# The sum of a token's row and its expert's second bias, made by GpSimd for 34 of 71 expert tiles

## The chip, the cores and the metric

The kernel runs on one core of a Trainium2 chip. The metric is the device time of one execution in microseconds (us); lower is better. Engine names in the profile: PE is TensorE (PEld its weight loads), DVE VectorE, ACT ScalarE, POOL GpSimd, SP SyncE, which only issues DMAs. A "q" behind a name (DVEq) is that engine's instruction queue.

## What is computed

64 sequences of 128 tokens, width 128, go through two layers; the last step is a mixture of 8 experts in which each token uses the expert of its largest router logit:

```python
    x = x + _L0_xattn_ref(ctx_1024, _layernorm(x, axis=-1), mask_BxS2_bk0, ...)
    x = x + _L0_ffn_ref(_layernorm(x, axis=-1), ...)
    x = x + _L1_xattn_ref(_layernorm(x, axis=-1), ctx_1024, L1_xattn_We, L1_xattn_W2)
    x = x + _L1_ffn_ref(_layernorm(x, axis=-1), ...)

    def _L1_ffn_ref(x, Wr, br, W1, b1, W2, b2):
        ...
        logits = xf @ Wr.T + br
        expert_idx = jnp.argmax(logits, axis=-1)
        h = jax.nn.relu(jnp.einsum('td,efd->etf', xf, W1) + b1[:, None, :])
        y = jnp.einsum('etf,edf->etd', h, W2) + b2[:, None, :]
        out = y[expert_idx, jnp.arange(xf.shape[0])]
```

The sum that the change moves is x + b2 of the token's expert, to which the second expert product is added later.

## The kernel before

**Rounds.** The program is written out in rounds j from -3 to 74; each engine has its own function `run` with its part of a round, in the order in which its queue executes it. In round j the cross-attention of sequence j is in several stages at once, and the dense parts of the later layers are done for groups of four sequences: rho = (j - 2) mod 4 tells which part of a group's work a round holds. From round 64 on (`tail`) no new sequence begins. Rounds 64 to 74 finish the last groups, and each holds three expert tiles besides.

**Expert tiles.** Tokens are scattered to DRAM sorted by expert (`sorted_rows`, by GpSimd's indirect DMA, line 810) and come back as 71 tiles of 128 tokens of one expert each (SyncE, line 502). The first 41 tiles come from sequences that are routed early; the other 30 are loaded when the last group's scatters have landed. One tile takes this way: VectorE's `prep` (lines 933 to 948) centres the tokens (L940), copies the expert's first weight and bias (L943) and adds the second bias to the row (L947, into one of eight buffers `xb2`); TensorE's `tile` transposes the tokens (L1641), makes h (L1647) and two tiles later y (L1655); ScalarE copies the transposed tokens (L554) and applies bias and relu (L559); VectorE's `finish` adds y and `xb2` into one of eight output buffers (L960); GpSimd's `store` sends the buffer to `out` by an indirect DMA (L800). `prep` works two tiles ahead of the number it is called with, `finish` and `store` two tiles behind it, so a tile's sum is made four places before it is used. In VectorE's queue the expert's number is read into a register by `look_up` (L931) one place earlier. Stores are numbered with semaphores, and the output buffer of tile k waits for the store of tile k - 8.

**The rstd chain.** Each round with layer norms in it makes one batch of 1/sqrt(var + eps): GpSimd writes the variances (`var_in`, L872), ScalarE takes ln and exp (L684, L687), GpSimd makes one Newton step (L881 to L887). In the tail it runs in rounds 64, 65, 66, 68, 69 and 72. ScalarE's `roots` stands ahead of the round's third expert tile in its queue. GpSimd's queue of a tail round is: variances, chain, in some rounds the centring `t_c` of a group (L835, L838), `xb` (L825), `ctx_now` (L820) or two scatters, and then the three stores.

After round 74 follow the tiles of `REST`, 32 and up, with nothing beside them.

Of the kernel before, what the change touches and what calls it, by code (L numbers as in the profile page):

```python
# [14 lines left out]
ALU = mybir.AluOpType  # L15
# [28 lines left out]
DEEP = 6  # L44
# [14 lines left out]
def whole(nc, x_res, ctx_res, ident, w1_all, w2_all, table, sent, padded, sorted_rows, out, x, ctx, mask,  # L59
# [3 lines left out]
    B, S, D = x.shape  # L63
# [5 lines left out]
    E, F = F1.shape[0], F1.shape[1]  # L69
# [6 lines left out]
    with ExitStack() as stack:  # L76
# [3 lines left out]
        def sem(name):  # L80
            return stack.enter_context(nc.semaphore(name))
# [115 lines left out]
        W1C, W2C, TOK = F + C, F + D, B * P  # L197
        out_rows = out.rearrange("b s d -> (b s) d")
        texp_i, trow_i = table["texp_i"], table["trow_i"]
        rows = x_res  # L200
# [6 lines left out]
        xb2 = [res[:, n * D:(n + 1) * D] for res in (q_t, o_n) for n in range(4)]  # L207
# [57 lines left out]
        sim_done = sem("sim_done")  # L265
# [6 lines left out]
        onT_done = sem("onT_done")  # L272
# [10 lines left out]
        second_in = sem("second_in")  # L283

        names = ("setup_d", "setup_t", "setup_c", "routed", "b_in", "wT_done", "w_copied", "w_taken", "tot_done", "tot_copied",
                 "a_bn", "a_mv", "fence_t", "lt_done", "lt_copied", "b_bn", "b_mv", "c_bn", "c_mv",
                 "ta_done", "amax_done", "step_done", "inv_done", "q1_done", "q2_done", "qT_done", "qt_copied",
                 "acc_done", "ya_done", "xb2_done", "x2_done", "tb_done", "tbT_done", "tb_copied",
                 "ctx_taken", "ctxT_done", "ctx_copied", "ke_done", "ke_copied", "v2_done",
# [2 lines left out]
                 "lmax_done", "ge_done", "cand_done", "cmax_done", "oh_done", "rank_done", "place_done", "gsum_done",  # L292
                 "own_done", "before_done", "slot_done", "staged")
        s = {n: sem("m_" + n) for n in names}
        tile_names = ("w1_set", "t_set", "T_done", "t_copied", "h_done", "relu_done", "y_done", "xb_set", "fin")
        se = {n: sem("e_" + n) for n in tile_names}
        out_sent = [sem(f"e_out_sent{n}") for n in range(STORES)]
        ld = [sem(f"e_ld{n}") for n in range(DEEP)]
# [7 lines left out]
        LAST = B + 10  # L306
# [86 lines left out]
        def group(g, inside):  # L393
            return inside or 0 <= g < NG
# [6 lines left out]
        def chain(j, inside):  # L401
            if inside or j <= B + 2:
                return j + 4
            return max([B + 6] + [n for at, n in CHAINS.items() if at <= j])

        def after(eng, name, g, inside):

            if inside or g >= 0:
                eng.wait_ge(s[name], g + 1)

        def grp(res, g, w=slice(0, D)):
            return res[:, bass.ds(G * g, G), w]
# [4 lines left out]
        TAIL, PLACES = B, 3  # L417
        TOTAL_AT, PAD_AT = 4 * (EARLY + 2) + 3, 4 * (NG + 1) + 3

        def tail(j, inside):  # L420
            return not inside and j >= TAIL

        def tile_no(j, place):

            return PLACES * (j - TAIL) + place - 1
# [3 lines left out]
        def has_tile(k):  # L429
            return 0 <= k < T  # L430

        def past(eng, name, k):
            if k >= 0:
                eng.wait_ge(se[name], k + 1)

        def flat(ap):
            return ap.rearrange("p a d -> p (a d)")
# [91 lines left out]
        def _(act):  # L529
# [18 lines left out]
            def tile(k, four=0, inside=False):  # L548
                if inside or has_tile(k + 1):

                    past(act, "T_done", k + 4 * four + 1)
                    if k == -1:
                        act.wait_ge(lo_done, B)
                    nc.scalar.activation(t_t[:, (k + 1) % 4, :], ps_t[(k + 1) % 2], ACT.Copy).then_inc(se["t_copied"], 1)  # L554
                if inside or has_tile(k):

                    past(act, "h_done", k + 4 * four)
                    for c in range(C):
                        last = nc.scalar.activation(h_t[k % 4][:, c, :], ps_h[k % 2][:, c * P:(c + 1) * P], ACT.Relu,  # L559
                                                    bias=w1_now[k % 4][:, F + c:F + c + 1])  # L560
                    last.then_inc(se["relu_done"], 1)
# [197 lines left out]
        def _(pool):  # L759
# [35 lines left out]
            def store(k):  # L795
                if has_tile(k - 2):

                    past(pool, "fin", k - 2)
                    n = (k - 2) % STORES
                    nc.gpsimd.indirect_dma_start(  # L800
                        out=out_rows,
                        out_offset=bass.IndirectOffsetOnAxis(ap=rows[:, k - 2, D + 2:D + 3].bitcast(U32), axis=0),
                        in_=o_now[:, n, :], in_offset=None, bounds_check=TOK - 1,
                        oob_is_err=False).then_inc(out_sent[n], 16)

            def scatter(g, lanes, inside):

                after(pool, "staged", g, inside)
                for i in lanes:
                    nc.gpsimd.indirect_dma_start(  # L810
                        out=sorted_rows, out_offset=bass.IndirectOffsetOnAxis(ap=idx[:, i:i + 1], axis=0),
                        in_=stage[:, i, :], in_offset=None).then_inc(sent[i // 2], 16)

            def run(j, par, rho, g, inside, pos, turn):
# [13 lines left out]
                if rho in (1, 2) and (inside or 0 <= g - 2 < NG - 1):  # L828
                    scatter(g - 2, (2 * rho - 2, 2 * rho - 1), inside)
                def centred(j, g):  # L830

                    after(pool, "tcT_done", g - 2, inside)
                    after(pool, "x3_done", g - 1, inside)
                    pool.wait_ge(rs_ready, chain(j, inside))
                    nc.gpsimd.tensor_tensor(t_c[:, :, :], grp(x_res, g - 1),  # L835
                                            stat_c[:, :, 0:1].to_broadcast([P, G, D]), ALU.subtract).then_inc(s["cc_done"], 1)
                    after(pool, "cc_done", g - 1, inside)
                    nc.gpsimd.tensor_tensor(t_c[:, :, :], t_c[:, :, :],  # L838
                                            rstd[:, j % 2 if tail(j, inside) else 1 - par, 28:28 + G].unsqueeze(2).to_broadcast([P, G, D]),
                                            ALU.mult).then_inc(s["tc_done"], 1)  # L840
# [61 lines left out]

                if rho == 2 and tail(j, inside) and group(g - 1, inside):
                    centred(j, g)
                if tail(j, inside):
                    store(tile_no(j, 0))
                    store(tile_no(j, 1))
                    if g - 2 == NG - 1 and rho == 0:
                        pool.wait_ge(padded, 16 * E)
                        scatter(g - 2, (0, 1), inside)  # L910
                    store(tile_no(j, 2))
                    if g - 2 == NG - 1 and rho == 0:
                        scatter(g - 2, (2, 3), inside)
                if not inside and 0 <= j < len(lots) - 3:
                    nc.gpsimd.memset(ctx_res[:, packed[j + 3], :], 0.0).then_inc(ctx_zeroed, 1)

            run(-3, 1, 3, -3, False, -3, 0)
            nc.gpsimd.memset(v_x[:, :, :, DH:DH + 1], 1.0).then_inc(setup_g, 1)
            nc.gpsimd.memset(v_c[:, :, :, DH:DH + 1], 1.0).then_inc(setup_g, 1)
            run(-2, 0, 0, -2, False, -2, 0)  # L920
            rounds_written_out(run)
            for k in REST:
                store(k)

        @block.vector
        def _(dve):
# [6 lines left out]
            def prep(k):  # L933
                if has_tile(k + 2):

                    n, e = (k + 2) % 4, number[k + 2]
                    past(dve, "T_done", k - 2)
                    dve.wait_ge(ld[(k + 2) % DEEP], 16 * ((k + 2) // DEEP + 1))
                    row = rows[:, k + 2, :]
                    nc.vector.tensor_scalar(t_now[:, n, :], row[:, 0:D], row[:, D:D + 1], row[:, D + 1:D + 2],  # L940
                                            ALU.subtract, ALU.mult).then_inc(se["t_set"], 1)
                    past(dve, "relu_done", k - 2)
                    nc.vector.tensor_copy(w1_now[n], flat(w1_all[:, bass.ds(e, 1), :])).then_inc(se["w1_set"], 1)  # L943
                    past(dve, "fin", k - 6)
                    if k == 2:
                        dve.wait_ge(onT_done, B)
                    nc.vector.tensor_tensor(xb2[(k + 2) % 8], row[:, 0:D], flat(w2_all[:, bass.ds(e, 1), F:W2C]),  # L947
                                            ALU.add).then_inc(se["xb_set"], 1)

            def finish(k):  # L950
                if has_tile(k - 2):

                    n = (k - 2) % STORES
                    if k - 2 >= STORES:
                        dve.wait_ge(out_sent[n], 16 * ((k - 2) // STORES))
                    if k == 2:
                        dve.wait_ge(pv_done, 2 * B)
                    past(dve, "xb_set", k - 2)
                    past(dve, "y_done", k - 2)
                    nc.vector.tensor_tensor(o_now[:, n, :], ps_y[k % 2], xb2[(k - 2) % 8], ALU.add).then_inc(se["fin"], 1)  # L960

# [948 lines left out]
```

## Time and profile before

| | |
|---|---|
| time, median of 3 runs | 921.79 us (919.71 to 922.56) |
| time of the profiled execution | 918.84 us |
| its span | 917.0 us |
| busy: PE, DVE, ACT, POOL | 96%, 81%, 75%, 48% |
| instructions of POOL | 1020 |
| granted TensorE clock | 0.999 of full |

The profile is of one execution. Its span runs from the first to the last recorded instruction; the 1.84 us between span and time lie around it. A busy share is a mean over the whole span: the expert tiles begin only near 747 us, and the engines' shares there are others. A time in a row is counted from the start of the span.

### The profile page before, as it was taken

Reading aid. Unit: us, or ns where it says so; the run is one execution under the profiler, and the core shown is the slowest. Engines: PE = TensorE matmul, PEld = TensorE weight load, DVE = VectorE, ACT = ScalarE, POOL = GpSimd, SP = SyncE. Lnnn points to the kernel's source line nnn. Section 1 sums busy time; section 2 is a strip of 40 time slices with the busy share of each in tenths; the row PEclk is TensorE's granted clock in tenths of the full one; section 3 lists DMA queues with packets and bytes.
Section 4 is the critical chain, followed back from the end, with each engine's and each line's share of the span. In section 5 each row is a group of like instructions: output and inputs, shape, how many; then the busy total and the mean of one; then the engine's idle time right before and its main releaser. Section 6 shows DMA issues by size and latency. Waiting matters only on the chain.

```text
span 917.0 us, 34057 instructions
## 1 busy us (share of the span) xinstructions
PE 882.9 (96%) x12822; PEld 782.1 (85%) x12822; DVE 747.0 (81%) x2654; ACT 686.8 (75%) x1671; POOL 437.0 (48%) x1020
## 2 busy tenths in 40 slices
PE   7999999999999999999999999999999989999997
PEld 6788888888888888888888888888888778898996
DVE  5667888888888888889888888898889878877553
ACT  4887778787878787878787878787877766776664
POOL 4422434354535453545354535453545355777554
PEclk9999999999999999999999999999999999999999
DMA  6753000000000000000000000000000023164310
GB/s 190 204 132 73 3 3 2 2 14 3 14 2 15 3 14 2 14 3 15 2 15 3 14 3 13 3 15 2 15 3 13 3 64 78 46 123 99 93 49 22
DMA packets 45206, 31.66 MB, mean 35 GB/s; under 512 B 11555, under 2 KB 40166, under 8 KB 45046
## 3 DMA queue, kind: packets, MB, share of 16 engines
q1 hardware_dynamic: 39398, 19.93, 9.2%
q0 software_dynamic: 4320, 8.50, 2.9%
q8 instruction: 105, 1.72, 0.8%
q10 hardware_dynamic: 1328, 1.06, 0.5%
q14 instruction: 55, 0.45, 0.2%
HBM read 17.75 MB, written 12.17 MB: 33 GB/s over the span
## 4 chain that ended last, share of the span: by engine, by line
PE 80%; DVE 11%; issue 2%; POOL 2%; DMA 1%; ACT 1%; SPq 1%; DVEq 0%; POOLq 0%; ACTq 0%
PE ps L1781 12%; PE ps L1733 11%; PE ps L1666 9%; PE ps L1706 6%; PE ps L1474 6%; PE ps L1476 6%; PE ps L1475 6%; PE ps L1655 5%; PE ps L1647 5%; PE ps L1805 4%; DVE sumsq L1286 2%; PE ps L1527 1%; PE ps L1551 1%; PE ps L1521 1%; PE ps L1676 1%
## 5 line engine op out<-in xcount | busy, mean ns | idle before, releaser
L1781 PE MATMUL ps<-qT_all,kT_all 64*64 64x128 f32 x4096 | 129.8, 273 | 8.3 <-DVE o_n L1378 6.6
L706 ACT ACTIVATE prob<-ps,neg_shift 128x512 f32<-128x512 f32 x128 | 80.9, 682 | 62.5 <-PE ps L1781 62.5
L1733 PE MATMUL ps<-v_x,prob 128*64 128x65 f32 x2048 | 126.2, 225 | 0.2 <-ACT probs L626 0.2
L1781 PEld LDWEIGHTS ps<-qT_all,kT_all 64*64 64x64 f32 x4096 | 110.8, 133 | 16.4 <-DVE o_n L1378 9.3
L1733 PE MATMUL ps<-v_c,prob 128*64 128x65 f32 x2048 | 123.0, 222 | 0.0
L1398 DVE TENSOR_TENSOR qk_hat<-ps,rstd 128x512 f32<-128x512 f32 x168 | 106.2, 683 | 19.4 <-POOL rstd L887 19.0
L1286 DVE TENSOR_REDUCE sumsq<-qk_hat 128x8 f32<-128x512 f32 x168 | 106.9, 675 | 18.3 <-ACT qk_hat L639 17.8
L1474 PE MATMUL ps<-w_hi,xc_hi 128*128 128x512 f32 x272 | 113.9, 419 | 0.8 <-POOL xc_lo L853 0.8
L881 POOL TENSOR_TENSOR rs_t<-rs_y 128x32 f32<-128x32 f32 x73 | 17.7, 243 | 201.5 <-ACT rs_y L687 201.5
L1733 PEld LDWEIGHTS ps<-v_x,prob 128*64 128x64 f32 x2048 | 103.6, 138 | 11.8 <-issue 11.3
L1476 PE MATMUL ps<-w_hi,xc_lo 128*128 128x512 f32 x272 | 107.4, 395 | 0.0
L1475 PE MATMUL ps<-w_lo,xc_hi 128*128 128x512 f32 x272 | 107.2, 394 | 0.0
L1733 PEld LDWEIGHTS ps<-v_c,prob 128*64 128x64 f32 x2048 | 103.6, 138 | 0.0
L639 ACT ACTIVATE qk_hat<-ps 128x512 f32<-128x512 f32 x168 | 97.0, 608 | 7.4 <-PE ps L1476 1.4
L1666 PE MATMUL ps<-ident,qk_hat 128*128 128x128 f32 x672 | 95.2, 277 | 3.1 <-DVE qk_hat L1398 2.7
L800 POOL DMA_INDIRECT out_dram<-prob,x_res x71 | 72.0, 1014 | 43.1 <-DVE prob L960 28.2
L1666 PEld LDWEIGHTS ps<-ident,qk_hat 128*128 128x128 f32 x672 | 74.1, 141 | 15.0 <-issue 10.0
L706 ACT ACTIVATE prob<-ps,mask_now 128x512 f32<-128x512 f32 x128 | 80.6, 685 | 0.7 <-PE ps L1781 0.7
L810 POOL DMA_INDIRECT sorted_rows<-stage,idx x64 | 71.8, 1121 | 15.9 <-issue 14.6
L896 POOL TENSOR_TENSOR x_b<-x_res,lno_b 128x128 f32<-128x128 f32 x64 | 33.7, 526 | 94.2 <-DVE x_res L1417 94.2
L1655 PE MATMUL ps<-w_all,kT_all 128*128 x568 | 74.7, 275 | 0.0
L1706 PE MATMUL ps<-wo_sb,o_t 128*128 128x128 f32 x512 | 69.8, 279 | 1.5 <-issue 1.5
(241 smaller groups left out, 2207.4 us busy)
## 6 DMA issues: line engine op xcount, KB each, us to landing
x_res<-sorted_rows SPq DMA_DIRECT2D x71, 65.5 KB
w_all<-in_L_ffn_W_dram SPq DMA_DIRECT2D x16, 256.0 KB, 5.6
sorted_rows<-fill SPq DMA_DIRECT2D x8, 327.5 KB
out_dram<-prob,x_res POOLq DMA_INDIRECT x71
sorted_rows<-stage,idx POOLq DMA_INDIRECT x64, 2.4
ctx_res<-in_ctx_dram SPq DMA_DIRECT2D x8, 115.5 KB
x_res<-in_x_dram SPq DMA_DIRECT2D x1, 768.0 KB
sorted_rows<-fill SPq DMA_DIRECT2D x1, 524.0 KB, 5.2
```

The lines of the kernel that those rows point to most:

```text
L639: nc.scalar.activation(sq[:, n * INNER:(n + 1) * INNER], ps_qk[:, n, :], ACT.Square).then_inc(sq_done, 1 if n == 0 or fresh(pos + 1) else 2)
L706: nc.scalar.activation(prob[:, n // 2, n % 2 * INNER:(n % 2 + 1) * INNER], ps_s[n], ACT.Exp, bias=(mask_now[:, par:par + 1] if n > 1 else ...
L1286: nc.vector.reduce_sum(sumsq[:, n * H:(n + 1) * H], sq[:, n * INNER:(n + 1) * INNER].rearrange("p (h d) -> p h d", d=DH), AX).then_inc(ss_ ...
L1398: nc.vector.tensor_tensor(qk_hat[:, n * INNER:(n + 1) * INNER].rearrange("p (h d) -> p h d", d=DH), ps_qk[:, n, :].rearrange("p (h d) -> p ...
L1474: nc.tensor.matmul(dst, tok_hi, w_hi[:, w:w + INNER], start=True, stop=False)
L1475: nc.tensor.matmul(dst, tok_hi, w_lo[:, w:w + INNER], start=False, stop=False)
L1476: return nc.tensor.matmul(dst, tok_lo, w_hi[:, w:w + INNER], start=False, stop=True)
L1655: last = nc.tensor.matmul(ps_y[k % 2], h_t[(k - 2) % 4][:, c, :], flat(w2_all[:, bass.ds(e, 1), c * P:(c + 1) * P]), start=c == 0, stop=c ...
L1666: last = nc.tensor.transpose(ps_qk[:, n, t * P:(t + 1) * P], qk_hat[:, n * INNER + t * P:n * INNER + (t + 1) * P], ident[:, :])
L1706: last = nc.tensor.matmul(ps_o(j, inside), o_t[:, t * P:(t + 1) * P], wo_sb[:, t, :], start=t == 0, stop=t == PAIRS - 1)
L1733: last = nc.tensor.matmul(dst[half:half + DH, :], prob[:, kt, col + half:col + half + DH], v, start=kt == 0, stop=kt == 1)
L1781: last = nc.tensor.matmul(ps_s[2 * kt + half][key:key + DH, cols], keys, q_t[rows, cols], start=True, stop=True)
```

## The change

GpSimd gets a function `with_bias(k)`: for the tiles 0 to 33 it waits for the loaded rows and for the tile that last used the buffer, reads the expert's number into a register and makes the sum. In a tail round it is called behind each of the three stores, for the tile that lies four after the stored one; the sum of tile 0 is made ahead of them in round 64. VectorE's `prep` makes the sum only from tile 34 on, with a semaphore of its own, `xb_more`, and `finish` waits for the one or the other. Buffers, order of tiles and all other work are as before.

```diff
-                 "a_bn", "a_mv", "fence_t", "lt_done", "lt_copied", "b_bn", "b_mv", "c_bn", "c_mv",
+                 "a_bn", "a_mv", "lt_done", "lt_copied", "b_bn", "b_mv", "c_bn", "c_mv",
...
-        tile_names = ("w1_set", "t_set", "T_done", "t_copied", "h_done", "relu_done", "y_done", "xb_set", "fin")
+        tile_names = ("w1_set", "t_set", "T_done", "t_copied", "h_done", "relu_done", "y_done", "xb_set", "xb_more", "fin")
...
+        BY_POOL = PLACES * (LAST + 1 - TAIL) + 1
+
+        def biased(eng, k):
+
+            if 0 <= k < BY_POOL:
+                eng.wait_ge(se["xb_set"], k + 1)
+            elif k >= BY_POOL:
+                eng.wait_ge(se["xb_more"], k + 1 - BY_POOL)
...
+            def with_bias(k):
+                if has_tile(k) and k < BY_POOL:
+
+                    pool.wait_ge(ld[k % DEEP], 16 * (k // DEEP + 1))
+                    past(pool, "fin", k - 8)
+                    if k == 4:
+                        pool.wait_ge(onT_done, B)
+                    e = pool.value_load(texp_i[0:1, k:k + 1], min_val=0, max_val=E - 1)
+                    nc.gpsimd.tensor_tensor(xb2[k % 8], rows[:, k, 0:D], flat(w2_all[:, bass.ds(e, 1), F:W2C]),
+                                            ALU.add).then_inc(se["xb_set"], 1)
...
+                if not inside and j == TAIL:
+                    pool.wait_ge(sim_done, 4 * B)
+                    with_bias(0)
                 if tail(j, inside):
                     store(tile_no(j, 0))
+                    with_bias(tile_no(j, 0) + 2)
                     store(tile_no(j, 1))
+                    with_bias(tile_no(j, 1) + 2)
                     if g - 2 == NG - 1 and rho == 0:
                         pool.wait_ge(padded, 16 * E)
                         scatter(g - 2, (0, 1), inside)
                     store(tile_no(j, 2))
+                    with_bias(tile_no(j, 2) + 2)
...
-                    past(dve, "fin", k - 6)
-                    if k == 2:
-                        dve.wait_ge(onT_done, B)
-                    nc.vector.tensor_tensor(xb2[(k + 2) % 8], row[:, 0:D], flat(w2_all[:, bass.ds(e, 1), F:W2C]),
-                                            ALU.add).then_inc(se["xb_set"], 1)
+                    if k + 2 >= BY_POOL:
+                        past(dve, "fin", k - 6)
+                        nc.vector.tensor_tensor(xb2[(k + 2) % 8], row[:, 0:D], flat(w2_all[:, bass.ds(e, 1), F:W2C]),
+                                                ALU.add).then_inc(se["xb_more"], 1)
...
-                    past(dve, "xb_set", k - 2)
+                    biased(dve, k - 2)
```

## Rows read from the trace of the kernel before

**Rows 1.** Busy us by engine (with instruction counts), granted clock, in stretches of the span.

```profile
775.00:800.00 25.00, 22.15 (x195) 20.55 (x194) 20.78 (x72) 17.65 (x69) 19.42 (x27) 1.00 0.20 55
...
850.00:875.00 25.00, 25.00 (x227) 25.00 (x226) 14.42 (x55) 17.15 (x67) 11.64 (x13) 1.00 0.37 95
```

**Rows 2.** Waits, 765 to 800 us: engine and line, releaser, total us, times, longest.

```profile
ACT rs_ln L684 <- POOL var_in L872: 2.8, 2, 2.2
...
PE ps L1641 <- DVE xc_hat L940: 1.3, 2, 0.8
```

**Rows 3.** Chain that ended last, 765 to 815 us: start, us, what.

```profile
796.99 0.23 POOL var_in L872
...
798.04 1.16 PE ps L1647 x8
```

**Rows 4.** ScalarE's timeline: start, us, line, operation, in brackets the idle time before.

```profile
797.24 0.23 ACT L684 ACTIVATE rs_ln<-var_in 128x32 f32<-128x32 f32 x1 [2.17 <-POOL var_in L872]
...
818.76 0.26 ACT L554 ACTIVATE xc_t<-ps 128x128 f32<-128x128 f32 x1
```

**Rows 5.** GpSimd's timeline, 764 to 834 us, columns as before.

```profile
764.90 0.25 POOL L887 TENSOR_TENSOR rstd<-rs_t,rs_y 128x32 f32<-128x32 f32 x1
765.64 1.04 POOL L800 DMA_INDIRECT out_dram<-prob,x_res  x1 [0.48 <-issue]
...
768.30 0.98 POOL L800 DMA_INDIRECT out_dram<-prob,x_res  x1 [0.30 <-issue]
769.28 0.23 POOL L872 TENSOR_TENSOR var_in<-stat_a,var_add 128x4 f32<-128x4 f32 x1
771.18 0.24 POOL L881 TENSOR_TENSOR rs_t<-rs_y 128x32 f32<-128x32 f32 x1 [1.67 <-ACT rs_y L687]
...
784.15 1.20 POOL L825 TENSOR_TENSOR xb<-x_res,bias_b 128x512 f32<-128x512 f32 x1
785.52 0.99 POOL L810 DMA_INDIRECT sorted_rows<-stage,idx  x1 [0.17 <-issue]
...
814.21 0.97 POOL L800 DMA_INDIRECT out_dram<-prob,x_res  x1 [1.20 <-DVE prob L960]
...
833.84 1.03 POOL L810 DMA_INDIRECT sorted_rows<-stage,idx  x1 [0.80 <-DVE idx L1232]
```

**Rows 6.** TensorE's timeline, 819 to 850 us (instructions of one line merged).

```profile
819.52 1.06 PE L1647 MATMUL ps<-xc_t,w_more 128*128 128x128 f32 x8
...
833.14 0.33 PE L1641 MATMUL ps<-ident,xc_hat 128*128 128x128 f32 x1 [0.56 <-issue]
...
840.01 0.33 PE L1641 MATMUL ps<-ident,xc_hat 128*128 128x128 f32 x1 [0.92 <-DVE xc_hat L940]
...
849.55 0.27 PE L1641 MATMUL ps<-ident,xc_hat 128*128 128x128 f32 x1
```

**Rows 7.** VectorE's timeline, 746 to 784 us.

```profile
746.72 0.46 DVE L940 TENSOR_SCALAR xc_hat<-x_res 128x128 f32<-128x128 f32 x1 [1.28 <-DMA x_res<-sorted_rows]
...
747.43 0.28 DVE L947 TENSOR_TENSOR qT_all<-x_res,w_all 128x128 f32<-128x128 f32 x1
747.64 0.28 DVE L1308 BATCH_NORM_STATS2 o<-ps 128x6 f32<-128x128 f32 x1
...
750.28 0.43 DVE L1143 TENSOR_SCALAR q_bf<-q_round 128x512 bf16<-128x512 f32 x1
...
783.59 2.06 DVE L1143 TENSOR_SCALAR q_bf<-q_round 128x512 bf16<-128x512 f32 x1
```

**Rows 8.** GpSimd's groups by form over the span: busy us, mean ns, idle before.

```profile
L896 POOL TENSOR_TENSOR x_b<-x_res,lno_b 128x128 f32<-128x128 f32 x64 | 33.7, 526 | 94.2 <-DVE x_res L1417 94.2
```

**Rows 9.** Register loads of VectorE's queue at line 931: duration ns min/median/max.

```profile
L931 DVEq TENSOR_LOAD <-table_texp_i x71: 298/304/957, 745.1 to 901.5; - x71
```

**Rows 10.** SyncE's timeline, 800 to 860 us.

```profile
842.39 16.85 SPq L502 DMA_DIRECT2D x_res<-sorted_rows  x15
```

**Rows 11.** DMA issues by line: KB each, median us from issue to landing.

```profile
tb_t<-in_L_xattn_We_dram SPq DMA_DIRECT2D x1, 64.0 KB, 2.1
```

## The prediction, made before the changed kernel ran

> **What bounds the kernel now.** I read the busy shares by stretch first. In the last stretch of pure expert tiles TensorE is busy all the time; in 775 to 800 us, where three expert tiles a round are woven into the last dense groups, it is at 22.15 of 25 us, VectorE at 20.78 and GpSimd at 19.42 [rows 1]. GpSimd's average over the whole kernel (48%) says nothing about this place. Next the waits of 765 to 800 us: ScalarE's logarithm of the rstd chain waits 2.8 us for GpSimd's var_in, 2.2 us of it at once, and TensorE waits 1.3 us for VectorE's centred tokens [rows 2]. Then the chain that ended last: it walks through var_in on GpSimd at 796.99, ln and exp on ScalarE after its wait of 2.17 us, and the next tile's weight product on TensorE at 798.04 [rows 3, 4]. The last question is what GpSimd does ahead of that var_in, and its timeline answers it: from the var_in of round 66 at 769.28 to the one of round 69 at 796.99 it goes from one instruction straight to the next [rows 3, 5]. Its only real waits there are the 1.67 us at 771.18 and a ScalarE round trip of 0.7. The 0.30 us marked "issue" between two indirect DMAs is no free time; each pair of them has it, whatever else happens. It meets VectorE again only at 814.21, where it waits 1.20 us for a finished tile.
>
> So in rounds 66 to 69 GpSimd ends last, at rounds 70 to 72 it has about 0.9 us in hand (1.20 at 814.21 less the usual 0.30 [rows 5]), and before 763 and from 828 to 840 VectorE is late: TensorE has gaps of 0.56 and 0.92 us there [rows 6]. From 840 on TensorE alone counts.
>
> **What is taken away.** 34 additions on VectorE (L947). One takes 0.28 us in its row, but the next instruction starts 0.21 after it (747.43 to 747.64), so each is worth 0.21 [rows 7]: 34 x 0.21 = 7.1 us of VectorE. It counts only where VectorE is late. Before 763 it starts the first stores about 0.5 us earlier: five additions are worth 1.05, and a wait for TensorE in their middle eats half; this is an estimate from the same rows. From 828 to 840 six additions are 1.3 us and the two gaps of TensorE are 1.48 [rows 6]; I take 1.0. In between, other engines end last, and it buys nothing.
>
> **What is added.** On GpSimd 34 additions of 128x128 f32, with a register load each. The nearest row of that addition is x_b, the same form with two SBUF inputs: 526 ns mean [rows 8]. What it adds to the queue is another number. A short tensor instruction (0.25 us at 764.90) is followed by an indirect DMA 0.74 us after its own start; a long one (1.20 at 784.15) is followed after 0.17 [rows 5]. So an addition of about 0.5 takes 0.74 before the next store and removes the 0.30 gap: 0.44. The third of each round mostly goes ahead of a tensor instruction, which follows a DMA with no gap (768.30 + 0.98 = 769.28): 0.53. Sum 1.4 a round if the register load hides. On VectorE's queue that load is 304 ns [rows 9], and two of them in the open held VectorE for 1.28 us ahead of 746.72 [rows 7], though the row puts it down to a DMA. So the load costs between 0 and 0.64 each. Since tensor instructions follow a DMA without a gap, the queue runs ahead, and I take nearly the lower end: 0.5 an addition in all, 1.5 us a round. Bounds 1.2 and 3.2 a round; a gain is excluded, for no row shows GpSimd doing two things at once. The waits on the loaded rows and on the tile eight before cost nothing: a store just ahead has already waited for the tile four before.
>
> **Where it lands.** Behind an addition in the queue stand the stores and the scatters of the round, and the next round's var_in, the rstd chain and t_c. Round 64: four additions after 757.04, when GpSimd is waiting for VectorE's statistics up to 762.38; free. Round 65: var_in at 769.28 - 0.5 + 1.5 = 770.3; ScalarE is ready for it at 770.5, and the rs_t at 771.18 hardly moves [rows 5]; 0. Rounds 66, 67, 68: 3 x 1.5 = 4.5 us, all of it in the var_in of round 69. TensorE is only about 0.1 us from waiting there, as its product at 798.04 starts right behind ScalarE's copy [rows 3]. Delay 4.5. Rounds 69, 70, 71: another 4.5, less the 0.9 in hand: the var_in of round 72 is 8.1 late. TensorE has 0.5 there (ScalarE's copy ends at 819.02, the product starts at 819.52) [rows 4, 6]: delay 7.6. VectorE's gain from 828 to 840 takes off 1.0: 6.6. Then the end of the routing: nine additions of rounds 72 to 74 stand ahead of the last scatter, 4.5 less the 0.5 that the scatter at 833.84 waits for VectorE beyond the usual [rows 5]: 8.1 + 4.0 = 12.1 us late. The load of tile 41 is issued at 842.39 behind it [rows 10], so at 854.5; 64 KB have landed in 2.1 us [rows 11], in other rows in up to 3.1: 856.6. VectorE needs 0.34 for it, and TensorE wants it at 849.55 + 6.6 = 856.2 [rows 6]: 0.8 more. Sum: 4.5 + 4.5 - 0.9 - 0.5 - 1.0 + 0.8 = +7.4 us.
>
> The profiled execution has a span of 917.0 and a time of 918.84, so 926.2 for the changed kernel; the median of the runs shown, 921.79, stands 2.95 above the profiled execution, and I carry that over: 921.79 + 7.4 = 929.2. With 1.2 us a round the sum is 6 x 1.2 - 2.4 = +4.8 (no wait for the load), with 1.8 it is 8.4 and about 2 for the load, +10.4. The new wait of VectorE, on an addition by GpSimd, stands ahead of the last addition of each tile, with the preparation of later tiles queued behind it. An addition is issued after the store of the tile four before; with GpSimd some 8 us late, the sum for tile 25 comes about 1.4 us after VectorE asks for it. That is 0 to 1.4 on top and in the range.
>
> **The shared port.** The q_bf conversion on VectorE took 2.06 us at 783.59 while GpSimd's xb addition ran from 784.15 to 785.35; its like at 750.28 took 0.43 [rows 5, 7]. So a VectorE instruction can be held for all of a GpSimd one. The Trainium skill, SBUF — State Buffer, section "SBUF: two separate sides", says that the two engines share a port pair as an exclusive lock, for VectorE instructions with two SBUF inputs or in a two-port mode: the trace agrees at this place. By that rule each moved addition can hold VectorE for up to its own length, and the change would give back its 1.5 us of gain; the sum would be 8.9 in place of 7.4. The rows alone leave open how many of the additions meet such an instruction: none of the sum above needs it, and both values lie inside the forecast.
>
> **Rivals.** (1) GpSimd's register load lies open. Each addition then costs 0.44 + 0.64, 3.2 a round. The var_in of round 66 is 1.45 late already, the sum is 1.45 + 6 x 3.2 - 2.4 = 18.3, and the load of tile 41 comes some 6 us after that: +24, 946 us. For it: the two open loads on VectorE. Against: the queue running ahead of a 0.97 us DMA. (2) Faster: GpSimd's additions fit into time that I count as busy, above all the 0.30 issue gaps, and VectorE's relief decides. The gaps of TensorE that VectorE causes are 1.3 in rounds 66 to 69 [rows 2], 0.56 and 0.92: 2.8 us, so 919.0. The mechanism is VectorE's queue getting shorter at the places where TensorE waits for xc_hat, and it decides from a price of under 0.4 us a round, 0.13 an addition. For it: VectorE is busier than GpSimd by the shares. Against: a tensor instruction never disappeared in GpSimd's queue, and VectorE's gain at 787 and 795 is of no use while var_in at 796.99 ends last. (3) Price and gain cancel: 0.4 us a round to 0.8 at most, or the lag of GpSimd is soaked up by waits that I don't see; 921.8. (4) That the additions aren't moved can't be: each stands in its engine's queue.
>
> **How the numbers follow.** Within 0.3% is 2.8 us; a measurement of this kernel can tell no less from no change. My forecast, GpSimd ending last, at +3 to +12: 0.64. Rival 1, anywhere above 12: 0.10. Rival 3: 0.13. Rival 2: 0.13. So slower 0.74, same 0.13, faster 0.13. The range leaves out rival 2 and most of rival 1 and reaches over rival 3: 920 to 938; the upper end holds a register load half in the open.
>
> **What would show it.** In the profile after: GpSimd rows for the additions with 0.45 to 0.55 us, three between stores; the distance of the var_in of round 66 to that of round 69 at 32 us in place of 27.7; ScalarE waiting some 3 us for var_in in round 68 and more in 69, where it waited 0.6 and 2.2; TensorE under 21 of 25 us busy in 775 to 800; VectorE without L947 before 842 and with new idle time put down to GpSimd; the load of tile 41 near 854; the last 50 us unchanged at 1.9 us a tile. Wrong would be: GpSimd waiting for VectorE at most stores, var_in no later than before, or a distance of additions and stores that shows the register load in the open.

## The result

The changed kernel takes 926.56 us, median of 5 runs (925.68 to 928.20), where the kernel before takes 921.04 on the same chip (919.71 to 922.56). The ratio is 1.0067, with a 95% interval of 1.0053 to 1.0081: 5.5 us slower. Run again beside other kernels it gave 926.47 and a ratio of 1.0071 [1.0056, 1.0086].

The profiled execution of the changed kernel took 928.20 us with a span of 926.5, which is 9.5 more than the span of before, and more than the medians differ. Part of it has nothing to do with the change: the var_in of round 64, ahead of the first addition on GpSimd, is at 754.48 in place of 751.98. All profiles of this study differ by up to 3.8 us at that point (751.5 to 755.3), some with a granted clock of 0.88 or 0.93 in the first 25 us and some with 1.00. So two profiles are compared here by **the tail**: from the start of the var_in of round 64 (the row with `stat_c`, 751.98 in the profile of before) to the end of the span. It is 165.0 us before and 172.0 after: +7.0.

This start is not quite free of the change. VectorE's first additions stand ahead of the statistics that this var_in needs, and without them it comes 0.4 us sooner, counted from the var_in before it. In the kernel before:

```profile
749.68 0.21 POOL L866 TENSOR_TENSOR var_in<-o_stat,var_add 128x1 f32<-128x1 f32 x1
751.98 0.75 POOL L872 TENSOR_TENSOR var_in<-stat_c,var_add 128x4 f32<-128x4 f32 x1 [2.10 <-DVE stat_c L1154]
```

and in the changed kernel:

```profile
752.58 0.20 POOL L886 TENSOR_TENSOR var_in<-o_stat,var_add 128x1 f32<-128x1 f32 x1
754.48 0.55 POOL L892 TENSOR_TENSOR var_in<-stat_c,var_add 128x4 f32<-128x4 f32 x1 [1.69 <-DVE stat_c L1179]
```

The distance is 2.3 us in the four profiles whose VectorE makes the first additions and 1.9 in the nine others. So against the kernel before, a tail of one of the nine shows 0.4 too much: the change cost 6.6 us inside the profile and not 7.0. Where this counts below, both numbers stand. Times "put back" have the 2.9 us between 749.68 and 752.58 taken off.

Busy us by engine in stretches of the changed kernel, columns as in [rows 1]:

```profile
775.00:800.00 25.00, 20.49 (x167) 19.50 (x166) 19.27 (x62) 13.83 (x54) 20.96 (x29) 0.93 0.22 59
800.00:825.00 25.00, 24.31 (x218) 22.97 (x217) 16.08 (x62) 16.93 (x66) 20.86 (x30) 1.00 0.30 70
825.00:850.00 25.00, 20.80 (x186) 19.57 (x185) 18.40 (x65) 15.07 (x55) 21.05 (x30) 1.00 0.69 110
850.00:875.00 25.00, 25.00 (x227) 25.00 (x226) 14.67 (x56) 17.14 (x66) 16.03 (x16) 1.00 0.35 95
```

TensorE is down to 20.49 us in 775 to 800 us, against the 22.15 of [rows 1], and GpSimd is at 21 us in all three stretches. VectorE is less busy than before, and from 850 on nothing has changed for TensorE. One number is new: the granted clock of 0.93 in the first line.

GpSimd's timeline, with the var_in of rounds 66, 68, 69 and 72, one round of stores with the additions between, and the last scatter:

```profile
772.29 0.22 POOL L892 TENSOR_TENSOR var_in<-stat_a,var_add 128x4 f32<-128x4 f32 x1
...
775.72 1.03 POOL L809 DMA_INDIRECT out_dram<-prob,x_res  x1 [0.49 <-issue]
776.78 0.47 POOL L823 TENSOR_TENSOR o_n<-x_res,w_all 128x128 f32<-128x128 f32 x1
777.42 1.12 POOL L809 DMA_INDIRECT out_dram<-prob,x_res  x1 [0.16 <-issue]
778.56 0.47 POOL L823 TENSOR_TENSOR qT_all<-x_res,w_all 128x128 f32<-128x128 f32 x1
779.20 0.99 POOL L809 DMA_INDIRECT out_dram<-prob,x_res  x1 [0.17 <-issue]
780.21 0.42 POOL L823 TENSOR_TENSOR qT_all<-x_res,w_all 128x128 f32<-128x128 f32 x1
780.57 0.52 POOL L840 COPY ctx_now<-ctx_res 128x384 f32<-128x384 f32 x1
...
793.36 0.41 POOL L892 TENSOR_TENSOR var_in<-stat_c,var_add 128x4 f32<-128x4 f32 x1
```

```profile
803.03 0.23 POOL L892 TENSOR_TENSOR var_in<-stat_b,var_add 128x4 f32<-128x4 f32 x1
...
826.01 0.21 POOL L892 TENSOR_TENSOR var_in<-stat_c,var_add 128x4 f32<-128x4 f32 x1
...
850.00 1.03 POOL L830 DMA_INDIRECT sorted_rows<-stage,idx  x1 [0.30 <-issue]
```

An addition starts 0.02 us behind its store and the next store 0.16 behind it. Before, the var_in of rounds 66 and 69 were 27.7 us apart [rows 3, 5]; here it is 30.74. What waits for it, in ScalarE's and VectorE's rows of the waits from 745 to 860 us (engine and line, releaser, total us, times, longest):

```profile
ACT rs_ln L693 <- POOL var_in L892: 8.3, 4, 4.5
...
DVE prob L985 <- POOL qT_all L823: 2.0, 2, 1.3
...
DVE prob L985 <- POOL o_n L823: 1.4, 1, 1.4
```

ScalarE waits 8.3 us for var_in in this stretch, 4.5 at once, where it waited 3.8 and 2.2 in the kernel before. The two other rows are the new wait: VectorE asks for sums that GpSimd has not made, 3.4 us in three places. (When the changed kernel was profiled again, the wait of 1.4 was not there, and the tail was 172.3.) TensorE's timeline shows what it comes to (in brackets the idle time before):

```profile
794.60 1.61 PE L1672 MATMUL ps<-xc_t,w_more 128*128 128x128 f32 x8 [3.39 <-ACT xc_t L563]
...
827.05 1.16 PE L1672 MATMUL ps<-xc_t,w_more 128*128 128x128 f32 x8 [1.03 <-ACT xc_t L563]
...
845.69 0.33 PE L1666 MATMUL ps<-ident,xc_hat 128*128 128x128 f32 x1 [0.81 <-DVE xc_hat L966]
...
849.45 0.33 PE L1666 MATMUL ps<-ident,xc_hat 128*128 128x128 f32 x1 [1.63 <-DVE xc_hat L966]
```

The first two gaps are behind ScalarE's stalls of rounds 68 and 72; at both places TensorE did not wait in the kernel before.

### The profile page after: what moved, and what is told of

It reads as the page before. It is cut to its first block, busy times and chain, and to the rows that moved or that the text cites. A ratio compares the mean times of both kernels' runs of the same rounds, so it can differ in the third digit from the quotient of the medians.

```text
span 926.5 us, 34187 instructions
## 1 busy us (share of the span) xinstructions
PE 886.5 (96%) x12822; PEld 784.7 (85%) x12822; DVE 745.2 (80%) x2620; ACT 687.6 (74%) x1671; POOL 452.9 (49%) x1054
## 4 chain that ended last, share of the span: by engine, by line
PE 78%; DVE 11%; issue 3%; POOL 3%; DMA 1%; ACT 1%; POOLq 1%; SPq 1%; DVEq 0%; ACTq 0%
PE ps L1758 12%; PE ps L1806 11%; PE ps L1691 9%; PE ps L1731 6%; PE ps L1499 6%; PE ps L1501 6%; PE ps L1500 6%; PE ps L1672 5%; PE ps L1680 5%; PE ps L1830 4%; DVE sumsq L1311 2%; PE ps L1701 1%; PE ps L1552 1%; PE ps L1576 1%; PE ps L1546 1%
## 5 line engine op out<-in xcount | busy, mean ns | idle before, releaser
L1758 PEld LDWEIGHTS ps<-v_x,prob 128*64 128x64 f32 x2048 | 103.6, 138 | 11.9 <-issue 11.3
```

The source lines that it names most:

```text
L1758: last = nc.tensor.matmul(dst[half:half + DH, :], prob[:, kt, col + half:col + half + DH], v, start=kt == 0, stop=kt == 1)
```

## The experiments

The eleven runs were made in three sets, each on its own chip; each ratio is to the kernel before on the same chip, so ratios and tails are what to compare, and medians of two sets only roughly.

### Which part costs: GpSimd's queue, VectorE's relief, or the wait

**GpSimd adds for nothing.** VectorE keeps its additions and waits for nothing new.

```diff
+            def idle_addition(k):
+                if has_tile(k) and k < 34:
+                    pool.wait_ge(ld[k % DEEP], 16 * (k // DEEP + 1))
+                    past(pool, "fin", k - 8)
+                    e = pool.value_load(texp_i[0:1, k:k + 1], min_val=0, max_val=E - 1)
...
+                    nc.gpsimd.tensor_tensor(idle_sum[:, k % 8, :], rows[:, k, 0:D], flat(w2_all[:, bass.ds(e, 1), F:W2C]),
+                                            ALU.add).then_inc(s["fence_t"], 1)
...
                     store(tile_no(j, 0))
+                    idle_addition(tile_no(j, 0) + 2)
```

> The kernel before, in which VectorE keeps all its additions and waits for nothing new; GpSimd makes the same 34 additions at the same places of its queue into a buffer that nobody reads. Theory Q (the additions lengthen GpSimd's queue ahead of var_in and of the last scatters): 5 to 8 us slower than before, no faster than the changed kernel; the distance of the var_in of round 66 to that of round 69 is 30.5 to 31.5 us in place of 27.7. Theory W (what costs is VectorE waiting for a sum that GpSimd makes, 3.4 us in the changed profile): within 1 us of before.

Measured: 930.05 us, ratio 1.011 [1.0092, 1.0127], tail 174.2 us: 9.2 more than before, above the 5 to 8 that I expected. The var_in of rounds 66 and 69 are 30.6 us apart. So the additions alone cost more than the whole change, with no wait of VectorE for them; theory W falls as the main cause.

**Nobody adds.** The second bias is left out of the first 34 tiles.

```diff
-                    nc.vector.tensor_tensor(xb2[(k + 2) % 8], row[:, 0:D], flat(w2_all[:, bass.ds(e, 1), F:W2C]),
-                                            ALU.add).then_inc(se["xb_set"], 1)
+                    if k + 2 >= 34:
+                        past(dve, "fin", k - 6)
+                        nc.vector.tensor_tensor(...).then_inc(se["xb_set"], 1)
...
+                    other = xb2[(k - 2) % 8] if k - 2 >= 34 else rows[:, k - 2, 0:D]
```

> The kernel before without the additions for tiles 0 to 33 on any engine: the second bias is left out of the first 34 tiles, and finish adds the token's row alone. This is VectorE's relief with no price. Theory Q: GpSimd and TensorE end last from 769 us on, so 0.5 to 2 us faster than before. Rival (VectorE is the bound and the change could have paid): 3 to 5 us faster.

Measured: 919.02 us, ratio 0.9979 [0.9968, 0.9990], tail 163.2: 1.8 less, or 2.2 with the 0.4 us of the tail's start. VectorE's 7.1 us are worth some 2, even as a gift. And the two halves add up: 9.2 - 2.2 = 7.0 beside the 6.6 of the change. ScalarE and TensorE in this kernel:

```profile
ACT rs_ln L684 <- POOL var_in L872: 4.5, 3, 2.5
```

```profile
796.31 1.16 PE L1648 MATMUL ps<-xc_t,qk_hat 128*128 128x128 f32 x8 [1.46 <-ACT xc_t L554]
```

With VectorE relieved, TensorE waits 1.46 us at 796, where var_in ends last: that is where much of the rest of the gift goes.

**GpSimd writes for nothing and reads nothing.** As the idle additions, but a memset in their place:

```diff
-                    nc.gpsimd.tensor_tensor(idle_sum[:, k % 8, :], rows[:, k, 0:D], flat(w2_all[:, bass.ds(e, 1), F:W2C]),
-                                            ALU.add).then_inc(s["fence_t"], 1)
+                    nc.gpsimd.memset(idle_sum[:, k % 2, :], 0.0).then_inc(s["fence_t"], 1)
```

> The kernel before with 34 memsets of 128x456 f32 on GpSimd, about as long as the additions, with the register load, at the additions' places. A memset reads no SBUF. Theory Q: the queue is as long as with the idle additions, so 8 to 10 us slower than before, like they were (9.3). Theory P (two engines reading SBUF hold each other, and VectorE's longer instructions are what costs): at most 5 us slower, and VectorE's instructions are as short as before.

Measured: 929.15 us, ratio 1.0097 [1.0078, 1.0116], tail 174.9 us: 9.9 more. VectorE's additions in 745 to 850 us (count, busy us, mean ns), beside the memsets and then beside the idle additions:

```profile
L963 DVE TENSOR_TENSOR qT_all<-x_res,w_all 128x128 f32<-128x128 f32 x20 | 5.6, 280 | 0.0
...
L963 DVE TENSOR_TENSOR o_n<-x_res,w_all 128x128 f32<-128x128 f32 x16 | 4.5, 280 | 0.0
```

```profile
L964 DVE TENSOR_TENSOR qT_all<-x_res,w_all 128x128 f32<-128x128 f32 x20 | 7.2, 359 | 0.0
L964 DVE TENSOR_TENSOR o_n<-x_res,w_all 128x128 f32<-128x128 f32 x16 | 6.2, 386 | 0.0
```

VectorE's additions, which have two SBUF inputs, are held beside GpSimd's additions, which read SBUF, and not beside its memsets: 359 and 386 ns against 280. Beside the memsets every one of these rows takes 0.27 to 0.29 us; beside the idle additions 14 of the 36 take 0.48 to 0.54, about as long as an addition of GpSimd. (The Trainium skill, SBUF — State Buffer, section "SBUF: two separate sides", has VectorE instructions with two SBUF inputs held only by GpSimd instructions that read SBUF; these rows agree.) But the memsets do not free VectorE. Its centring of the tokens has one SBUF input; beside the memsets, beside the idle additions and in the kernel before, in 745 to 850 us:

```profile
L956 DVE TENSOR_SCALAR xc_hat<-x_res 128x128 f32<-128x128 f32 x36 | 17.6, 488 | 1.5 <-DMA x_res<-sorted_rows 1.3 <-issue 0.2
```

```profile
L957 DVE TENSOR_SCALAR xc_hat<-x_res 128x128 f32<-128x128 f32 x36 | 16.0, 443 | 1.3 <-issue 1.3
```

```profile
L940 DVE TENSOR_SCALAR xc_hat<-x_res 128x128 f32<-128x128 f32 x42 | 15.7, 375 | 1.3 <-DMA x_res<-sorted_rows 1.3
```

It takes 488 ns beside the memsets, even more than beside the additions. All instructions of `prep` together take VectorE 1.14 us a tile in the kernel before, 1.32 beside the additions and 1.26 beside the memsets. So this run takes away about a third of the hold and not all of it, and the loss is the same 9.9 against 9.2. A memset took 576 ns on the mean, somewhat more than the 496 of an idle addition; by length 9.9 x 496 / 576 is 8.5, and were all 34 x 0.08 us of the longer memsets lost, it would be 7.2. This third of the hold is then worth 0.7 to 2.0 us by my estimate. That most of the loss is the queue does not follow from this run; it follows from where the delay arises and from the runs on the order in the queue, below.

**Each sum twice**, in the changed kernel.

```diff
                     e = pool.value_load(texp_i[0:1, k:k + 1], min_val=0, max_val=E - 1)
+                    nc.gpsimd.tensor_tensor(idle_sum[:, k % 8, :], rows[:, k, 0:D], flat(w2_all[:, bass.ds(e, 1), F:W2C]), ALU.add)
```

> The changed kernel with each of GpSimd's 34 sums made twice, once into a buffer that nobody reads, with one register load. Theory Q: another 0.45 to 0.5 us an addition, 1.4 us a round: from the var_in of round 66 to that of round 69 35 us in place of 30.7, and 8 to 11 us on top of the changed kernel, 935 to 938. If the register load or a fixed cost of an addition is what counts, less than 4 us on top.

Measured: 939.63 us, ratio 1.021 [1.0189, 1.0231], tail 183.9: 11.9 more than the changed kernel for 34 additions, 0.35 each. The var_in of rounds 66 and 69 are 33.3 us apart, and TensorE waits 5.95 us behind the stall of round 68 (3.39 in the changed kernel). So the loss grows with the length of the queue, above the range that I gave at its upper end and with a smaller distance than I gave; it is not a fixed cost or the register load, for which less than 4 us more were expected.

### What the order in the queue does

**Third store later**, in the kernel before and in the changed one. All instructions stay; the last store of a round goes behind the next var_in, where GpSimd waits 0.7 us for ScalarE.

```diff
+                if tail(j, inside) and j > TAIL + 1:
+                    store(tile_no(j - 1, 2))
+                if chained(j, inside):
...
-                    store(tile_no(j, 2))
+                    if j == TAIL or j == LAST:
+                        store(tile_no(j, 2))
```

> The kernel before, only that in rounds 65 to 73 GpSimd makes the third store of a round after the var_in of the next round, while ScalarE takes the logarithm, and no more ahead of it. Theory Q: var_in of round 69 comes 2 to 4 us earlier against that of round 66's place, ScalarE's wait of 2.2 us there goes; TensorE was only 0.1 us short there, so 0 to 1.5 us faster than before. Rival (stores delay what they free, the output buffers, and VectorE waits for them): slower by 1 us or more, with waits of VectorE on the stores.

Measured: 919.58 us, ratio 0.9992 [0.9979, 1.0006], tail 164.7. Counted from the var_in of round 64, that of round 69 comes 1.6 us earlier, less than the 2 to 4 that I expected. ScalarE's wait for var_in falls from 3.8 us in 745 to 870 to 1.5, VectorE waits for no store, and the time is the same within the interval. In both kernels TensorE waits at these places for VectorE's centred tokens as well (0.77 us at 796.27, and 0.77 at 795.20 in the kernel before); that this is why the relief of var_in buys nothing is an argument, and no run tests it.

> The changed kernel, only that in rounds 65 to 73 GpSimd makes the third store of a round after the var_in of the next one. All additions stay on GpSimd; what changes is only what stands ahead of var_in. Theory Q: var_in of round 69 comes 2 to 3.5 us earlier against that of round 64 (48.5 us behind it in the changed profile), and from the var_in of round 64 to the span's end it is 168 to 170 us in place of 172.0; 922.5 to 925. Theory W (VectorE waiting for GpSimd's sums): the stores that are moved change nothing for the sums, so 926 to 928.

Measured: 924.47 us, ratio 1.0046 [1.0030, 1.0063], tail 169.7: 2.3 less than the changed kernel with the same instructions. The var_in of round 69 is 46.3 us behind that of round 64 in place of 48.6. Which work stands ahead of var_in sets a third of the loss, 2.3 of 6.6.

### The fall of the clock

Behind the gap of 3.39 us TensorE's granted clock read 0.50 for 2 us, which is 1.2 GHz, the lower of its two levels:

```profile
792.00:794.00 2.00, 0.00 (x0) 0.00 (x0) 1.93 (x7) 0.20 (x1) 1.44 (x3) 1.00 0.17 57
794.00:796.00 2.00, 1.40 (x8) 1.40 (x9) 1.00 (x8) 1.72 (x8) 1.12 (x5) 0.78 0.03 11
796.00:798.00 2.00, 2.00 (x10) 2.00 (x10) 0.00 (x0) 1.14 (x4) 1.92 (x2) 0.50 0.03 8
798.00:800.00 2.00, 2.00 (x15) 1.63 (x15) 1.75 (x5) 0.74 (x3) 1.67 (x4) 0.86 0.10 33
```

Some 1.7 us of full speed are missing there. Idle transposes in the gap:

```diff
+                    if k == 14:
+                        past(pe, "relu_done", 12)
+                        for i in range(24):
+                            nc.tensor.transpose(ps[:, 0, 0:P], ident[:, :], ident[:, :])
                     past(pe, "t_copied", k)
```

> The changed kernel with 24 idle transposes on TensorE ahead of the product of tile 14, in the place where it stood idle for 3.39 us and after which its granted clock read 0.78, 0.50 and 0.86 for 2 us each. Theory C (that fall of the clock cost 1.7 us of the loss, and comes from the gap): the clock stays at 1.00 there, and the time is 1.0 to 1.8 us below the changed kernel's 926.6. Rival (the time lost to the clock is hidden behind GpSimd's var_in of round 69 at 803, which ends last anyway): the clock stays at 1.00 and the time is within 0.5 us of the changed kernel's.

Measured: 924.86 us, ratio 1.0055 [1.0036, 1.0073]. The clock read 1.00 from 745 to 870, the gap ahead of the product shrank to 0.78, and a gap of 2.13 opened 10 us later, where the changed kernel has 0.43; the tail is 171.8, like the changed kernel's 172.0. Median and tail did not agree, so both kernels ran again side by side.

> The changed kernel itself, beside the one with idle transposes on the same chip: 925.5 to 927.5, ratio to before 1.006 to 1.0075.

Measured: 926.47 us, ratio 1.0071 [1.0056, 1.0086], tail 172.3, clock 0.76 and 0.50 behind a gap of 3.40.

> The changed kernel with the 24 idle transposes ahead of the product of tile 14, again, to be set against the changed kernel on the same chip. Theory C (the fall of TensorE's clock behind the 3.39 us gap costs time): 1.2 to 1.8 us below it. Rival (the time is hidden behind GpSimd's var_in of round 69): within 0.7 us of it; the first profile speaks for this, with 171.8 us from the var_in of round 64 to the end beside 172.0.

Measured: 927.06 us, ratio 1.0076 [1.0061, 1.0092], tail 172.2. The clock held where the transposes stood; in this profile it fell later, in the gap of 2.15 us ahead of 802.78. So no cost of the fall shows here: what TensorE does sooner after round 68 it waits for in round 69, for the next var_in. The only profile with the clock at 1.00 throughout is the first of these two, and its tail of 171.8 lies within 0.6 us of the three with a fall (172.0, 172.3 and 172.2). Its median of 924.86 is 1.7 below that of the changed kernel in the first measurement; the intervals of the two ratios overlap, and side by side the transposes gained nothing.

### Additions only where GpSimd has room

**Seven sums.** `BY_POOL = 7`, with the third store later:

> GpSimd makes the sums of the first 7 tiles only, those that it makes in rounds 64 and 65, where it waited for VectorE; VectorE makes the other 64; and the third store comes later as in e5. Theory Q: these seven cost nothing and give VectorE some 0.5 us before 763 us; 918.5 to 920.5, from the var_in of round 64 to the end 163.5 to 164.8 us (165.0 before, 164.65 with the third store later alone). If an addition on GpSimd hurts wherever it stands: 921 or more.

Measured: 919.30 us, ratio 0.9984 [0.9974, 0.9995], tail 163.7. The additions of rounds 64 and 65 cost nothing. Whether they give something can't be told from the time (0.9992 with the third store later alone, and the intervals overlap); the tail is 0.9 us shorter than that kernel's, or 1.3 with the 0.4 of its start. TensorE's largest gap from 745 to 870 is then 1.50 us at 841.56, ahead of a transpose that waits for VectorE, beside the last table.

**Seven and four.** In addition the sums of tiles 34 to 37, behind the last scatter.

```diff
-        BY_POOL = PLACES * (LAST + 1 - TAIL) + 1
+        BY_POOL, LATE = 7, range(34, 38)
...
                         scatter(g - 2, (2, 3), inside)
+                        for n in LATE:
+                            with_bias(n)
```

> The third store later, and GpSimd's sums only where its queue has room: tiles 0 to 6 in rounds 64 and 65, and tiles 34 to 37 right behind the last scatter, while VectorE makes the last table and TensorE waits 1.50 us for its centred tokens. Theory Q: nothing is delayed on GpSimd, four times 0.21 us less on VectorE there: 163.0 to 163.6 us from the var_in of round 64 to the end (163.7 with the seven alone), 917.5 to 919.5. If the load of tile 41 or GpSimd's sums come too late: 920 or more.

Measured: 916.74 us, ratio 0.9962 [0.9946, 0.9977], tail 163.1: 0.4% faster than the kernel before, and it leaves nothing out. The tail is 1.9 us shorter than before, or 2.3 with its start; the median is 3.4 below that of the kernel before on this chip (920.18). The profiled execution was the slowest of its six (918.25), and where the rest of the difference comes from is not traced. It rests on three edits (the third store later, the seven sums, the four sums); of these the first alone measured 0.9992 and the first two 0.9984. GpSimd's timeline of this kernel, with a store in ScalarE's time at 788.43 and the four sums behind the last scatter:

```profile
788.05 0.22 POOL L894 TENSOR_TENSOR var_in<-stat_c,var_add 128x4 f32<-128x4 f32 x1
788.43 1.02 POOL L811 DMA_INDIRECT out_dram<-prob,x_res  x1 [0.16 <-issue]
789.47 0.25 POOL L906 TENSOR_TENSOR rs_t<-rs_y 128x32 f32<-128x32 f32 x1
```

```profile
838.96 0.96 POOL L832 DMA_INDIRECT sorted_rows<-stage,idx  x1 [0.30 <-issue]
839.95 0.95 POOL L825 TENSOR_TENSOR qT_all<-x_res,w_all 128x128 f32<-128x128 f32 x2
840.87 1.00 POOL L825 TENSOR_TENSOR o_n<-x_res,w_all 128x128 f32<-128x128 f32 x2
842.04 1.01 POOL L811 DMA_INDIRECT out_dram<-prob,x_res  x1 [0.16 <-issue]
```

The wait for ScalarE ahead of rs_t is gone (789.47 follows the store at once). The gap of TensorE at the last table is 0.88 here and was 1.50 with the seven alone.

## Why the prediction was right

The forecast was +7.4 us on the profiled span. Measured were +6.6 inside the profile (+7.0 by the tail), +5.5 in the medians at first and +6.3 the second time; the forecast of 929.2 us lies 2.6 above the median. Step by step, put back by 2.9 us:

- **What bounds it** was right: GpSimd's queue ahead of var_in. The idle additions cost 9.2 us though VectorE kept all its work and waited for no sum, and with the third store behind var_in the changed kernel lost 2.3 us less.
- **The price of an addition** was 0.5 us, and the rows give less. Between rounds 66 and 69 nine additions lengthened the distance by 3.03 us while GpSimd's wait for ScalarE in round 66 shrank by 0.44: 3.5 us, 0.39 each, below even my 0.44 for an addition between two stores. The additions ran 0.47 us on the median, and the store behind one follows after 0.16, not after the 0.24 that I took from a shorter instruction.
- **The register load** hides behind the store, as assumed. It shows only in round 64, where four additions stand in a row (759.30 to 761.38) and start 0.69 to 0.70 apart with 0.23 to 0.28 between. Rival 1 fell.
- **Round 65**: the var_in of this round came 0.7 earlier (forecast 0.5), and the var_in of round 66 0.1 late (forecast 1.0). The rs_t behind it, which waits for ScalarE, was 0.3 early; forecast was no delay of it.
- **Rounds 68 and 69**: the var_in of round 69 was 3.1 late, forecast 4.5. The prediction had ScalarE wait some 3 us in round 68 and more in round 69; it waited 4.51 and 1.51 (0.58 and 2.17 before). So the stall that holds TensorE, 3.39 us, is that of round 68, one chain earlier than the one that the forecast was worked out from.
- **Round 72**: 5.1, forecast 8.1. From 69 to 72 only 1.9 came on top, where 4.5 less 0.9 was forecast: this is the step most off in its size. Nine additions at 0.39 are 3.5, less the 0.9 in hand from [rows 5] makes 2.6. Most of the other 0.7 was in hand as well: in the kernel before, the rs_t at 797.90 took 0.54 us where the changed kernel's takes 0.24, and the gap ahead of the store at 812.02 was 0.57 and not 0.30.
- **TensorE** was 4.6 late at the product of round 72 (827.05, before 819.52), forecast 7.6.
- **The last scatter and the load of tile 41** were 7.8 and 7.9 late (850.00, and 853.20 in place of 842.39), forecast 12.1. In the tail no load of these was waited for; the 0.8 was not paid.
- **VectorE's gain of 1.0 from 828 to 840** did not come, and this step failed. From round 72 to the end the delay grew from 4.6 to 6.6. VectorE waited 1.29 and 0.70 us for sums at 832 and 834, but at the start of the last table (`table_total`, 840.96 in place of 832.97) it was only 5.1 late: 0.5 had come on top. The other 1.5 came in the table itself. From `table_total` to `table_trow_i` VectorE took 7.66 us in place of 6.21, though it waited for no sum there, and TensorE's gaps for centred tokens were 0.81 + 1.63 in place of 0.92.

What made the table longer are rows that end when an instruction of GpSimd ends. VectorE and GpSimd in the changed kernel:

```profile
842.99 0.68 DVE L1001 TENSOR_SCALAR table_ntile<-table_ntile 128x8 f32<-128x8 f32 x1
843.70 0.50 DVE L1080 TENSOR_TENSOR table_ntile<-table_ntile,table_ntile_a 128x8 f32<-128x8 f32 x1
```

```profile
842.68 0.99 POOL L809 DMA_INDIRECT out_dram<-prob,x_res  x1 [0.16 <-issue]
843.69 0.48 POOL L823 TENSOR_TENSOR qT_all<-x_res,w_all 128x128 f32<-128x128 f32 x1
```

In the kernel before the same two took 0.25 and 0.17 us. The centring L966 at 841.14 (0.81, before 0.35) and L1025 at 848.11 (0.48, before 0.18) end within 0.1 us of the end of a GpSimd instruction too. Where GpSimd has no added work beside the table, it takes 5.9 to 6.5 us (five profiles: the kernel before, the third store later, nobody adds, and the two kernels with few sums); where it has, 6.9 to 8.3 (the eight others), with the idle additions (6.94) and the memsets (7.82) among them, whose VectorE waits for no sum. So the wait for sums is not what cost here: by these rows it is the hold, which the prediction had in its sentences on the shared port and left out of its sum. In the kernel with seven sums TensorE's gap is 1.50 us with a table of 6.52; this one is not explained.

So the errors, additions too dear, a relief that did not come and a hold left out, took each other away; the mechanism was right for the first 4.6 us, and that the total of 7.4 lies so near to 6.6 is in part luck.

The shared port thus cost the changed kernel some 1.5 us at its last table. Rival 2, VectorE's relief deciding, is priced by the kernel in which nobody adds: some 2 us, not 2.8, and only if the additions are free.

## What to carry to other kernels

Before work is moved to an engine with idle time, look at what stands behind it in that engine's queue in the very stretch: a mean of 48% and 19.4 of 25 us hid a queue in which nothing fitted any more, and 34 additions at 0.4 us each came back as 6.6 us of delay, 9.2 without VectorE's relief. The same work costs nothing where the queue waits for others: seven additions where GpSimd waited for VectorE, four behind its last urgent DMA, and a store in the time of a round trip to another engine together made the kernel 0.4% faster. A gift experiment, leaving the work out altogether, shows in one run what the relief could be worth at most: here some 2 us for 7.1 of busy time. And a stand-in that is meant to take one cause away must be checked in the trace: the memsets spared VectorE's additions and held its other instructions. Last, a point of the trace that is to serve as a common start has to lie ahead of every instruction that the edit touches.

## What the runs showed of the hardware

- A GpSimd addition of 128x128 f32 takes 0.47 us and, between two indirect DMAs, lengthens the queue by 0.35 to 0.4, since it takes the place of a 0.30 us gap between them. The register load for its address, 0.29 on the queue, hides behind a DMA of 0.97.
- VectorE's additions of a row and a bias, both in SBUF, took 0.27 to 0.29 us beside GpSimd's memsets and up to 0.54 beside its idle additions; the centring with one input was held beside both (means of 488 and 443 ns, 375 before).
- TensorE's granted clock fell to 0.50 of full in or behind gaps of 2.15, 2.77, 3.39, 3.40, 3.63, 3.79 and 5.95 us, in six profiles, and read 1.00 behind one of 2.13. The 2.15 and the 2.13 are the same gap in two profiles of one kernel, with tails of 172.2 and 171.8.
- The part of the kernel ahead of the expert tiles, which no edit touched, differed by 3.4 us in thirteen profiles (its last var_in before them at 741.2 to 744.6). Changes of a microsecond at the end are read better from a distance inside the profile than from its span.
